# The sums of V are made chunk by chunk, between the score stages, instead of four in a row at the head of a super-chunk

## The chip, the cores and the metric

One Trainium2 chip, 8 of its cores, each with one of the eight sequences of the batch; nothing is exchanged between them. The metric is the time of one execution in device microseconds, that of the slowest core. Engines: PE (TensorE) multiplies matrices, ACT (ScalarE) evaluates functions, DVE (VectorE) reduces and copies, POOL (GpSimd) issues part of the DMAs here, and SP issues the others. The engines run beside each other, each through its own instructions in order, and wait for each other through semaphores.

## The reference, cut to what matters

```python
xn = _layernorm(x)                       # x: 8 x 8192 x 1024, one of the 8 per core
q, k, v = proj(xn)                       # 16 heads of 64, 64 chunks of 128 tokens
s_intra = q @ k.T * scale                # inside a chunk: 128 x 128 per head
intra   = softmax(s_intra) @ v
k_means = k.mean(over a chunk); v_means = v.mean(over a chunk)
s_inter = q @ k_means.T * scale          # against the means of chunks 0..c
inter   = softmax(s_inter, causal) @ v_means
attn    = (intra + inter) @ wo.T + bo
ffn     = gelu((xn @ U1) @ V1 + b1) @ U2 @ V2 + b2
out     = x + attn + ffn
```

## The kernel before, in words

A core goes through its 8192 tokens in 16 super-chunks (`sc`) of 512 tokens, that is four chunks of 128 (`cc` = 0 to 3, `c = 4 * sc + cc`). Every engine's instructions stand in the order in which the Python code emits them with `pm.do(engine, instruction, waits, incs)`; "t" is PE, "v" DVE, "s" ACT, "y" SP and "g" POOL. A wait stops the engine and all that is emitted behind it for that engine.

In each super-chunk: the normalized x is transposed (L399, L408), the projections of q and k (L424, copied by ACT at L433) and of v (L443 and L451, copied by DVE at L457 into `v_tm`) follow. DVE then sums the next super-chunk's x (`emit_ln_sums`, L337 and L340; not in the last super-chunk) and makes the chunk means of k with 32 pairs of small instructions, 8 pairs for each chunk (L473 and L478, into `km_fm`).

**The sums of v** (L483 to L514) stand next. For each chunk two matmuls with a column of ones (L489, L494) make one row of 1024 sums in PSUM banks 6 and 7; ACT copies the two halves (L500, L503) into a row buffer; POOL issues two DMAs (L508, L511) that carry the row to partition c and to partition 64 + c of `vm_cm`. There are two row buffers, and they are no memory of their own: `vrow_slots` is partition 0 of `A1T` and partition 0 of `A2T`, the tiles that later hold the exponentials. Chunk 2 takes the buffer of chunk 0 again, so its matmuls wait for the DMAs of chunk 0 (`vrow_guard`), and chunk 3 likewise for those of chunk 1.

**P1** (`emit_p1`, called P1(cc) below) makes six banks of scores for one chunk (L542 for the scores inside the chunk, L570 for those against `km_fm`); its first matmul waits for `km_done[cc]`. ACT exponentiates (L553, L589), DVE sums (L557, L594), ACT takes two logarithms (L609, L611), and DVE makes `neglse` (L615). **The bounce** (`emit_lse_bounce`) transposes `neglse` on PE (L623), DVE makes two copies (L628, L631), and POOL sends them to DRAM and back as flat rows (L638, L641, then four times L653). **P2** (`emit_p2_av`) makes the transposed scores with the flat rows added, part 0 and part 1 with three banks each (L680 and L690, or L698 and L711); L690 and L698 wait for the flat rows. ACT exponentiates each bank into `A1T` (L722) or `A2T` (L728). Part 2, **AV**, multiplies with v (L754) and with `vm_cm` (L778) into banks 6 and 7, which DVE copies out (L790).

The order of emission is P1(0), bounce(0), the first FFN matmul (L807), then for each cc: P1(cc + 1), P2(cc) part 0, bounce(cc + 1), P2(cc) part 1, AV(cc). With cc = 3 there is no P1 and no bounce. P1, P2 and the bounce take their PSUM banks in turn from banks 0 to 5 (`pool_next`), and each use of a bank waits until the bank's last content was read. One turn of the loop takes 6 + 3 + 1 + 3 = 13 banks, so the third bank of part 1 is the one that the first exponential of part 0 has to free.

The exponentials of P2 wait for `vm_ready`, because they overwrite the row buffers: the counts of the two DMA semaphores after all four chunks. AV waits for `vm_ready` since it reads `vm_cm`. After the fourth AV come the layer norm of the next super-chunk, the GELU part of the FFN (L846, L854, L870) and the output (L900 to L924).

Of the kernel before, what the change touches and what calls it, by code (L numbers as in the profile page):

```python
# [71 lines left out]
def build_nc(nsc=NSC_FULL, debug=False):  # L72
# [98 lines left out]
    c_t = Ctr(nc, "c_t")  # L171
# [8 lines left out]
    d_vm = [Ctr(nc, "d_vm0"), Ctr(nc, "d_vm1")]  # L180
# [14 lines left out]
    for (dst, src) in ((ident, ident_c), (ident_b, identb_c), (ones2, ones2_c),  # L195
# [8 lines left out]
          waits=[c_v], incs=[(d_ffw, 16)])  # L204
# [18 lines left out]
          waits=[d_ffw], incs=[(c_v, 1)])  # L223
# [12 lines left out]
    for wi, (wsrc, dstT, scale_col) in enumerate(wlist):  # L236
        for fc in range(8):
# [4 lines left out]
                  waits=w_st, incs=[(d_st[slot], 16)])  # L242
            wts = [(d_st[slot], d_st[slot].n), (d_cst, d_cst.n),
                   (c_v, ev_after.get(("e", slot), dbg_v0))]
            for half in range(2):
                bank = B[slot * 2 + half]
                for eci in range(4):
# [6 lines left out]
                          waits=(wts if (half == 0 and eci == 0) else ()),  # L254
# [21 lines left out]
    with nc.Block("setup") as blk1:  # L276
# [7 lines left out]
          waits=[(c_v, setup_v)], incs=[(c_t, 1)])  # L284
    t_bias0 = c_t.n
    pm.do("g", dma("g", bias_r[0:8, :], bk_h.rearrange("(a t) -> a t", t=128)),
          waits=[(c_t, t_bias0)], incs=[(d_ffw, 16)])
    pm.do("t", lambda e: e.transpose(B[0][0:128, 8:16], bias_r[0:8, :], ident[0:8, 0:8]),
          waits=[(d_ffw, d_ffw.n)], incs=[(c_t, 1)])
# [3 lines left out]
          waits=[(c_t, t_bias1)], incs=[(c_v, 1)])  # L293
# [3 lines left out]
          waits=[(c_v, v_bias1)], incs=[(d_ffw, 16)])  # L297
    pm.do("t", lambda e: e.transpose(B[0][0:128, 16:48], bias_r[:], ident[0:32, 0:32]),
          waits=[(d_ffw, d_ffw.n), (c_v, v_bias1)], incs=[(c_t, 1)])
    pm.do("v", lambda e: e.tensor_copy(b1_f[:], B[0][:, 16:48]),  # L300
          waits=[c_t], incs=[(c_v, 1)])
# [11 lines left out]
    vm_ready = [(d_vm[0], 0), (d_vm[1], 0)]  # L313
# [63 lines left out]
    for sc in range(nsc):  # L377
# [3 lines left out]
        if sc + 1 < nsc:  # L381
# [5 lines left out]
                  waits=[x_guard[npar]], incs=[(d_xp[npar], 16)])  # L387
# [3 lines left out]
        for st in range(4):  # L391
            bks = (4, 5) if st % 2 else (6, 7)
            for half in range(2):
                bk = bks[half]
                w = [(c_v, ln_done[st]), bank_free[bk]]
                for eci in range(4):
# [7 lines left out]
                          waits=(w if eci == 0 else ()),  # L404
# [9 lines left out]
                      waits=[(c_t, bank_gen[bk]), xnfm_guard], incs=[(c_v, 1)])  # L414
# [3 lines left out]
        for (wT, dst, brow) in ((wqT, q_fm, bq_eff), (wkT, k_fm, bk_f)):  # L418
            for fc in range(8):
                bk = fc % 4  # L420
                w = [(c_v, xn_ready), bank_free[bk], (c_s, setup_s)]
                for ec in range(8):
# [6 lines left out]
                          waits=(w if ec == 0 else ()),  # L429
# [5 lines left out]
                      waits=[(c_t, bank_gen[bk]), kq_guard], incs=[(c_s, 1)])  # L435
                bank_free[bk] = (c_s, c_s.n)
        for st in range(4):
            for half in range(2):
                bk = (st * 2 + half) % 4
                w = [(c_v, xn_ready), bank_free[bk]]  # L440
                for ec in range(8):
# [7 lines left out]
                          waits=(w if ec == 0 else ()))  # L449
# [10 lines left out]
                      waits=[(c_t, bank_gen[bk]), kq_guard], incs=[(c_v, 1)])  # L460
# [19 lines left out]
                      waits=[c_v], incs=[(c_v, 1)])  # L480
            km_done.append(c_v.n)

        for cc in range(4):  # L483
            c = 4 * sc + cc
            vr = vrow_slots[cc % 2]
            w = [(c_v, v_done), bank_free[6], bank_free[7], vrow_guard[cc % 2],
                 hflat_guard, a_guard]
            pm.do("t", (lambda cc=cc: lambda e:
                        e.matmul(B[6][0:1, :], ones_col[:],  # L489
                                 v_tm[:, cc * 1024:cc * 1024 + 512],  # L490
                                 start=True, stop=True))(),
                  waits=w, incs=[(c_t, 1)])
            pm.do("t", (lambda cc=cc: lambda e:
                        e.matmul(B[7][0:1, :], ones_col[:],  # L494
                                 v_tm[:, cc * 1024 + 512:cc * 1024 + 1024],
                                 start=True, stop=True))(),
                  incs=[(c_t, 1)])
            bank_gen[6] = bank_gen[7] = c_t.n
            pm.do("s", (lambda vr=vr: lambda e:
                        e.activation(vr[0:1, 0:512], B[6][0:1, :], AF.Copy))(),  # L500
                  waits=[(c_t, c_t.n)], incs=[(c_s, 1)])
            pm.do("s", (lambda vr=vr: lambda e:
                        e.activation(vr[0:1, 512:1024], B[7][0:1, :], AF.Copy))(),  # L503
                  incs=[(c_s, 1)])
            bank_free[6] = bank_free[7] = (c_s, c_s.n)
            sw = [c_s.snap()]
            pm.do("g", (lambda c=c, vr=vr: lambda e:
                        e.dma_start(out=vm_cm[c:c + 1, :], in_=vr))(),  # L508
                  waits=sw, incs=[(d_vm[cc % 2], 16)])
            pm.do("g", (lambda c=c, vr=vr: lambda e:  # L510
                        e.dma_start(out=vm_cm[64 + c:65 + c, :], in_=vr))(),  # L511
                  incs=[(d_vm[cc % 2], 16)])
            vrow_guard[cc % 2] = (d_vm[cc % 2], d_vm[cc % 2].n)
        vm_ready = [(d_vm[0], d_vm[0].n), (d_vm[1], d_vm[1].n)]  # L514

        cix = lambda h: (h % 2) * 8 + h // 2
        grp_heads = [[h for h in range(16) if cix(h) // 4 == g] for g in range(4)]
# [143 lines left out]
        def emit_p2_av(cc, flat_v, part):  # L661
# [11 lines left out]
            for kind, g in gens:  # L673
                bk = pool_next()
                if kind == "i":
                    for qi, h in enumerate(grp_heads[g]):
                        base = (h % 2) * 64
                        fc = h // 2
                        pm.do("t", (lambda bk=bk, qi=qi, base=base, fc=fc,
                                    cc=cc: lambda e: e.matmul(  # L680
                                        B[bk][:, qi * 128:(qi + 1) * 128],
                                        k_fm[base:base + 64, fc * 512 + cc * 128:
                                             fc * 512 + cc * 128 + 128],
                                        q_fm[base:base + 64, fc * 512 + cc * 128:
                                             fc * 512 + cc * 128 + 128],
                                        start=(qi == 0), stop=False,
                                        skip_group_check=True))(),
                              waits=([bank_free[bk]] if qi == 0 else ()))
                    pm.do("t", (lambda bk=bk, g=g, fi=fi, o2=o2: lambda e:
                                e.matmul(B[bk][:], o2,  # L690
                                         fi[:, g * 512:(g + 1) * 512],
                                         start=False, stop=True,
                                         skip_group_check=True))(),
                          waits=[(d_lsl, flat_v)], incs=[(c_t, 1)])
                else:
                    par8 = g
                    pm.do("t", (lambda bk=bk, g=g, fb=fb, s4=s4: lambda e:
                                e.matmul(B[bk][:], s4,  # L698
                                         fb[:, g * 512:(g + 1) * 512],
                                         start=True, stop=False,  # L700
                                         skip_group_check=True))(),
                          waits=[bank_free[bk], (d_lsl, flat_v)])
                    hs = [h for h in range(16) if h % 2 == par8]
                    for j, h in enumerate(hs):
                        base = (h % 2) * 64
                        fc = h // 2
                        q8 = cix(h) % 8
                        sl = (q8 % 4) * 128
                        pb = 64 * (q8 // 4)
                        pm.do("t", (lambda bk=bk, sl=sl, pb=pb, base=base,  # L710
                                    fc=fc, cc=cc, ncj=ncj, j=j: lambda e: e.matmul(  # L711
                                        B[bk][pb:pb + ncj, sl:sl + 128],
                                        km_fm[base:base + 64,
                                              fc * 64:fc * 64 + ncj],
                                        q_fm[base:base + 64, fc * 512 + cc * 128:
                                             fc * 512 + cc * 128 + 128],
                                        start=False, stop=(j == 7),
                                        skip_group_check=True))(),
                              incs=([(c_t, 1)] if j == 7 else ()))
                if kind == "i":  # L720
                    pm.do("s", (lambda bk=bk, g=g: lambda e:
                                e.activation(A1T[:, g * 512:(g + 1) * 512],  # L722
                                             B[bk][:], AF.Exp))(),
                          waits=[(c_t, c_t.n), avd] + vm_ready,
                          incs=[(c_s, 1)])
                else:
                    pm.do("s", (lambda bk=bk, g=g: lambda e:
                                e.activation(A2T[:, g * 512:(g + 1) * 512],  # L728
                                             B[bk][:], AF.Exp))(),
                          waits=[(c_t, c_t.n), avd] + vm_ready,  # L730
                          incs=[(c_s, 1)])
                exp_done[(kind, g)] = c_s.n
                bank_free[bk] = (c_s, c_s.n)
# [5 lines left out]
            for h in [hh for hh in range(16) if hh % 2 == 0] + \  # L739
# [10 lines left out]
                if ci % 4 == 0:  # L750
# [9 lines left out]
                      waits=w)  # L760
# [37 lines left out]
                bank_free[abk] = (c_v, c_v.n)  # L798

        nl0 = emit_p1(0)  # L800
        fl0 = emit_lse_bounce(0, nl0)
        flat_v = {0: fl0}
        for rc in range(2):
# [16 lines left out]
        for cc in range(4):  # L820
            if cc + 1 < 4:
                nl = emit_p1(cc + 1)
            exp_done_st[0] = {}
            emit_p2_av(cc, flat_v[cc], 0)
            if cc + 1 < 4:
                flat_v[cc + 1] = emit_lse_bounce(cc + 1, nl)
            emit_p2_av(cc, flat_v[cc], 1)
            emit_p2_av(cc, flat_v[cc], 2)
# [164 lines left out]
```

How the kernel before makes its waits and increments, by code:

```python
            def run(engine):  # L51
                done = {}
                for (ek, waits, fn, incs) in self.steps:
                    if ek != eng_key:
                        continue
                    for (c, val) in waits:
                        if val > 0 and done.get(id(c), -1) < val:
                            engine.wait_ge(c.h, val)
                            done[id(c)] = val
                    instr = fn(engine)
                    for (c, k) in incs:
                        instr.then_inc(c.h, k)
```

## Time and profile before

| what | value |
|---|---|
| median of 3 runs | 3536.42 us (3533.74 to 3555.97) |
| the profiled execution: its time | 3534.85 us |
| the profiled execution: span of its slowest core (5) | 3533.3 us |
| spans of the 8 cores | 3524.1 to 3533.3 us |
| granted TensorE clock of the 8 cores | 0.782 to 0.788 |
| busy: PE, ACT, DVE, POOL | 2437.2, 1208.0, 1056.0, 298.1 us |
| one super-chunk | about 207 to 215 us |

All times in rows are microseconds from the start of the span of core 5. The time of an execution is 1.55 us more than the span, which leaves out what lies before the first and after the last instruction.

### The profile page before, as it was taken

What the parts mean: (1) busy time and instruction counts of PE and PEld (TensorE: products, weight loads), DVE (VectorE), ACT (ScalarE), POOL (GpSimd) and SP (SyncE); (2) the same over time, 40 slices, a digit from 0 to 9 for tenths busy, and PEclk for the clock granted to TensorE, in tenths of its full rate; (3) what the DMA queues carried; (4) which work ended last, traced back from release to release, by engine and by line L of the source; (5) the groups of instructions that cost most, each with busy time, mean ns of one, the idle gap of its engine ahead of it and who ended that gap; (6) DMA issues with size and microseconds to landing.
All of it is one profiled execution on the core that took longest, in us unless ns stands there. A gap on an engine that the chain in (4) does not pass through costs nothing.

```text
span 3533.3 us, 41208 instructions; the slowest of 8 cores (3524.1 to 3533.3 us)
## 1 busy us (share of the span) xinstructions
PE 2437.2 (69%) x14403; PEld 1137.3 (32%) x14403; DVE 1056.0 (30%) x2444; ACT 1208.0 (34%) x2080; POOL 298.1 (8%) x558
## 2 busy tenths in 40 slices
PE   1267858676785767768576785867768576785867
PEld 0224333332333323333332333323333232333333
DVE  2432241413214141331513224141331513224141
ACT  0126143242513325252332614324252342614333
POOL 1101010100101010010100101010010100101010
PEclk9986959687695977859687695977859687695978
DMA  7400101000010100101010010100101010010000
GB/s 119 85 1 2 48 3 48 2 19 30 3 48 3 48 2 13 37 2 49 3 43 6 2 48 3 48 2 13 37 2 48 2 34 16 2 48 3 24 2 25
DMA packets 45429, 86.05 MB, mean 24 GB/s; under 512 B 17292, under 2 KB 24108, under 8 KB 44972
## 3 DMA queue, kind: packets, MB, share of 16 engines
q1 hardware_dynamic: 18348, 67.24, 5.4%
q0 software_dynamic: 26880, 16.18, 3.3%
q8 instruction: 120, 1.97, 0.2%
q14 instruction: 81, 0.66, 0.1%
HBM read 62.03 MB, written 34.60 MB: 27 GB/s over the span
## 4 chain that ended last, share of the span: by engine, by line
PE 56%; DVE 20%; issue 8%; ACT 7%; DMA 2%; POOL 1%; DVEq 1%; ACTq 0%; POOLq 0%
PE B L424 14%; PE B L870 7%; PE B L900 7%; PE B L443 7%; PE B L846 6%; DVE kcol L473 4%; DVE z L557 4%; PE B L807 3%; DVE km_fm L478 2%; PE B L690 2%; ACT v_tm L356 2%; DVE out_st L924 2%; DVE stats L337 2%; PE B L680 2%; PE B L754 2%
## 5 line engine op out<-in xcount | busy, mean ns | idle before, releaser
L870 PE MATMUL B<-H_rot,U 128*128 128x512 bf16 x1024 | 320.3, 399 | 134.9 <-ACT H_rot L854 133.8
L854 ACT ACTIVATE H_rot<-B,b_f 128x512 bf16<-128x512 f32 x512 | 349.2, 689 | 115.0 <-PE B L846 114.9
L433 ACT ACTIVATE q_fm<-B,bq_eff 128x512 bf16<-128x512 f32 x128 | 88.2, 689 | 730.6 <-PE B L424 730.6
L900 PE MATMUL B<-woT,attn_fm 128*128 128x512 bf16 x1024 | 242.6, 379 | 136.1 <-DVE out_st L924 111.2
L846 PE MATMUL B<-P_fm,V 128*128 128x512 bf16 x1024 | 332.3, 415 | 0.0
L623 PE MATMUL B<-identity,neglse 128*32 128x128 f32 x64 | 23.8, 371 | 401.3 <-DVE neglse L615 401.3
L457 DVE CAST v_tm<-B 128x512 bf16<-128x512 f32 x128 | 88.5, 691 | 678.6 <-PE B L451 678.6
L424 PE MATMUL B<-xn_fm,wqT 128*128 128x512 bf16 x1024 | 257.5, 418 | 31.9 <-DVE xn_fm L408 31.9
L443 PE MATMUL B<-wvT,xn_fm 128*128 128x512 bf16 x1024 | 243.0, 380 | 0.0
L424 PE MATMUL B<-xn_fm,wkT 128*128 128x512 bf16 x1024 | 223.6, 379 | 0.0
L553 ACT ACTIVATE B<-B,cvals 128x512 f32<-128x512 f32 x256 | 158.5, 659 | 182.1 <-PE B L542 181.9
L722 ACT ACTIVATE A1T<-B 128x512 bf16<-128x512 f32 x256 | 146.8, 592 | 161.4 <-PE B L690 161.4
L924 DVE TENSOR_TENSOR out_st<-B,x_buf 128x512 f32<-128x512 f32 x128 | 88.5, 692 | 376.7 <-PE B L917 376.7
L508 POOL DMA_DIRECT2D vm_cm<-A1T x32 | 16.0, 499 | 2122.1 <-ACT A1T L503 1986.7
L690 PE MATMUL B<-H_rot,ones 2*128 2x512 bf16 x256 | 147.3, 575 | 68.6 <-DMA Q_fm<-lse_scr 57.8
L870 PEld LDWEIGHTS B<-H_rot,U 128*128 128x128 bf16 x1024 | 101.4, 101 | 278.2 <-issue 173.2
L790 DVE CAST attn_fm<-B 128x512 bf16<-128x512 f32 x128 | 82.4, 686 | 341.1 <-PE B L778 341.1
L900 PEld LDWEIGHTS B<-woT,attn_fm 128*128 128x128 bf16 x1024 | 91.1, 97 | 265.2 <-issue 174.5
L557 DVE TENSOR_REDUCE z<-B 128x4 f32<-128x512 f32 x256 | 164.9, 685 | 16.8 <-ACT B L553 14.9
L589 ACT ACTIVATE B<-B,cvals 128x8 f32<-128x8 f32 (+42 forms) x128 | 58.1, 454 | 322.1 <-DVE z L557 322.1
L886 DVE CAST Q_fm<-B 128x512 bf16<-128x512 f32 x32 | 20.6, 685 | 483.6 <-PE B L870 483.6
L424 PEld LDWEIGHTS B<-xn_fm,wqT 128*128 128x128 bf16 x1024 | 107.1, 106 | 177.2 <-issue 79.8
(104 smaller groups left out, 3241.9 us busy)
## 6 DMA issues: line engine op xcount, KB each, us to landing
x_buf<-L_attn_hidden_states SPq DMA_DIRECT2D x16, 2048.0 KB, 10.2
out<-out_st SPq DMA_DIRECT2D x64, 512.0 KB, 2.7
V<-L_ffn_V POOLq DMA_DIRECT2D x1, 2048.0 KB, 23.9
U<-L_ffn_U POOLq DMA_DIRECT2D x1, 2048.0 KB, 40.3
H_rot<-L_attn_wq POOLq DMA_DIRECT2D x8, 256.0 KB, 4.0
H_rot<-L_attn_wk POOLq DMA_DIRECT2D x8, 256.0 KB, 3.8
H_rot<-L_attn_wv POOLq DMA_DIRECT2D x8, 256.0 KB, 3.8
H_rot<-L_attn_wo POOLq DMA_DIRECT2D x8, 256.0 KB, 3.8
```

What stands on the lines that cost most here:

```text
L424: e.matmul(B[bk][:], wT[:, ec * 1024 + fc * 128: ec * 1024 + fc * 128 + 128], xn_fm[:, ec * 512:(ec + 1) * 512], start=(ec == 0), stop=(ec ...
L443: e.matmul(B[bk][:], xn_fm[:, ec * 512 + st * 128: ec * 512 + st * 128 + 128], wvT[:, ec * 1024 + half * 512: ec * 1024 + half * 512 + 512 ...
L473: e.reduce_sum(kcol[:], k_fm[:, fc * 512 + cc * 128: fc * 512 + cc * 128 + 128], axis=AX.X))(),
L553: e.activation(B[bk][:], B[bk][:], AF.Exp, bias=cvals[:, 5:6]))(),
L557: e.reduce_sum(z1[:, 4 * g:4 * g + 4], B[bk][:].rearrange("p (a b) -> p a b", a=4), axis=AX.X))(),
L690: e.matmul(B[bk][:], o2, fi[:, g * 512:(g + 1) * 512], start=False, stop=True, skip_group_check=True))(),
L722: e.activation(A1T[:, g * 512:(g + 1) * 512], B[bk][:], AF.Exp))(),
L846: pm.do("t", (lambda bk=bk, g=g, rc=rc: lambda e: e.matmul(B[bk][:], V1[:, rc * 4096 + g * 128:rc * 4096 + g * 128 + 128], P_fm[:, rc * 51 ...
L854: pm.do("s", (lambda bk=bk, g=g: lambda e: e.activation(H_rot[:, (g % 4) * 512:(g % 4) * 512 + 512], B[bk][:], AF.Gelu_apprx_tanh, bias=b1 ...
L870: pm.do("t", (lambda gq=gq, rc=rc: lambda e: e.matmul(B[6 + rc][:], U2[:, gq * 256 + rc * 128:gq * 256 + rc * 128 + 128], H_rot[:, (gq % 4 ...
L900: e.matmul(B[bk][:], attn_fm[:, ec * 512 + st * 128: ec * 512 + st * 128 + 128], woT[:, ec * 1024 + half * 512: ec * 1024 + half * 512 + 512],
L924: lambda e: e.tensor_tensor(out_st[:, slot * 1024 + half * 512: slot * 1024 + half * 512 + 512], B[bk][:], xb[:, st * 1024 + half * 512: s ...
```

## The change

The loop over the four sums of v becomes a function `emit_vsum(cc)`. It is called for chunk 0 right after P1(0), and for chunk cc + 1 right after P1(cc + 1), ahead of P2(cc) part 0. `vm_latest[0]` holds the counts of the DMA semaphores after the newest call, and the exponentials of P2 wait for these. `vm_ready`, for which AV waits, is now that of its own chunk. Nothing is computed otherwise, and the number of instructions of each kind stays.

```diff
-        for cc in range(4):
+        vm_latest = [[(d_vm[0], 0), (d_vm[1], 0)]]
+
+        def emit_vsum(cc):
             c = 4 * sc + cc
             vr = vrow_slots[cc % 2]
             w = [(c_v, v_done), bank_free[6], bank_free[7], vrow_guard[cc % 2],
...
             vrow_guard[cc % 2] = (d_vm[cc % 2], d_vm[cc % 2].n)
-        vm_ready = [(d_vm[0], d_vm[0].n), (d_vm[1], d_vm[1].n)]
+            vm_latest[0] = [(d_vm[0], d_vm[0].n), (d_vm[1], d_vm[1].n)]
+            return vm_latest[0]
...
                     pm.do("s", (lambda bk=bk, g=g: lambda e:
                                 e.activation(A1T[:, g * 512:(g + 1) * 512],
                                              B[bk][:], AF.Exp))(),
-                          waits=[(c_t, c_t.n), avd] + vm_ready,
+                          waits=[(c_t, c_t.n), avd] + vm_latest[0],
                           incs=[(c_s, 1)])
                 else:
                     pm.do("s", (lambda bk=bk, g=g: lambda e:
                                 e.activation(A2T[:, g * 512:(g + 1) * 512],
                                              B[bk][:], AF.Exp))(),
-                          waits=[(c_t, c_t.n), avd] + vm_ready,
+                          waits=[(c_t, c_t.n), avd] + vm_latest[0],
                           incs=[(c_s, 1)])
...
         nl0 = emit_p1(0)
+        vm_ready_cc = {0: emit_vsum(0)}
         fl0 = emit_lse_bounce(0, nl0)
...
         for cc in range(4):
             if cc + 1 < 4:
                 nl = emit_p1(cc + 1)
+                vm_ready_cc[cc + 1] = emit_vsum(cc + 1)
+            vm_ready = vm_ready_cc[cc]
             exp_done_st[0] = {}
             emit_p2_av(cc, flat_v[cc], 0)
```

## Rows read from the trace of the kernel before

**Rows 1.** The page: busy time, and the chain that ended last by engine.
```profile
PE 2437.2 (69%) x14403; PEld 1137.3 (32%) x14403; DVE 1056.0 (30%) x2444; ACT 1208.0 (34%) x2080; POOL 298.1 (8%) x558
PE 56%; DVE 20%; issue 8%; ACT 7%; DMA 2%; POOL 1%; DVEq 1%; ACTq 0%; POOLq 0%
```
**Rows 2.** Timeline of PE, head of the fifth super-chunk: start, length, instruction, [idle before].
```profile
1061.10 0.38 PE L489 MATMUL B<-v_tm,ones_col 128*1 128x512 bf16 x1 [1.05 <-DVE v_tm L457]
1068.13 0.58 PE L489 MATMUL B<-v_tm,ones_col 128*1 128x512 bf16 x1 [4.12 <-DMA vm_cm<-A1T]
...
1072.81 1.01 PE L542 MATMUL B<-k_fm,q_fm 64*128 64x128 bf16 x8 [1.25 <-DVE km_fm L478]
...
1094.16 0.37 PE L623 MATMUL B<-identity,neglse 128*32 128x128 f32 x1 [19.16 <-DVE neglse L615]
```
**Rows 3.** Timeline of DVE, the same stretch.
```profile
1067.55 0.29 DVE L473 TENSOR_REDUCE kcol<-k_fm 128x1 f32<-128x128 bf16 x1 [0.37 <-DVE stats L340]
...
1088.61 1.29 DVE L557 TENSOR_REDUCE z<-B 128x4 f32<-128x512 f32 x2
```
**Rows 4.** Timeline of PE, turn cc = 1 of this super-chunk, and L690 of cc = 3.
```profile
1112.48 1.03 PE L542 MATMUL B<-k_fm,q_fm 64*128 64x128 bf16 x8
...
1119.54 0.37 PE L623 MATMUL B<-identity,neglse 128*32 128x128 f32 x1 [1.58 <-DVE neglse L615]
...
1121.45 0.60 PE L698 MATMUL B<-Q_fm,sel 4*128 4x512 bf16 x1
1121.99 0.60 PE L711 MATMUL B<-q_fm,km_fm 64*18 64x128 bf16 x8
1122.52 1.49 PE L754 MATMUL B<-A1T,v_tm 128*64 128x128 bf16 x16
1123.94 0.67 PE L778 MATMUL B<-A2T,vm_cm 18*64 18x128 bf16 x16
1124.55 1.03 PE L542 MATMUL B<-k_fm,q_fm 64*128 64x128 bf16 x8
...
1140.16 0.58 PE L690 MATMUL B<-H_rot,ones 2*128 2x512 bf16 x1 [2.90 <-DMA Q_fm<-lse_scr]
```
**Rows 5.** Timeline of ACT: copies of v sums, then the turn of rows 4.
```profile
1062.29 0.57 ACT L503 ACTIVATE A1T<-B 1x512 bf16<-1x512 f32 x1
...
1069.23 0.59 ACT L500 ACTIVATE A1T<-B 1x512 bf16<-1x512 f32 x1 [4.06 <-PE B L494]
1069.73 0.57 ACT L503 ACTIVATE A1T<-B 1x512 bf16<-1x512 f32 x1
...
1118.74 0.29 ACT L611 ACTIVATE lnz<-z,cvals 128x16 f32<-128x16 f32 x1
1118.94 1.06 ACT L722 ACTIVATE A1T<-B 128x512 bf16<-128x512 f32 x2
1119.90 0.60 ACT L728 ACTIVATE A2T<-B 128x512 bf16<-128x512 f32 x1
```
**Rows 6.** Timeline of POOL: its DMA issues (start, length) in the same super-chunk.
```profile
1065.91 0.52 POOL L508 DMA_DIRECT2D vm_cm<-A1T  x1 [135.46 <-ACT A2T L503]
1066.42 0.53 POOL L511 DMA_DIRECT2D vm_cm<-A1T  x1
...
1070.83 0.49 POOL L508 DMA_DIRECT2D vm_cm<-A1T  x1 [2.94 <-ACT A1T L503]
1071.31 0.48 POOL L511 DMA_DIRECT2D vm_cm<-A1T  x1
...
1133.45 0.51 POOL L638 DMA_DIRECT2D lse_scr<-rows_cd  x1 [6.84 <-PE B L690]
```
**Rows 7.** The tile vm_cm: from issue to landing of its 128 DMAs.
```profile
DMA to landing us min/median/max: 1.5/1.6/2.8
```
**Rows 8.** Line L553, its table loads: ns, first and last start.
```profile
L553 ACT ACT_TABLE_LOAD  x15: 1283/1283/1283, 449.8 to 3394.5; - x15
```
**Rows 9.** Timeline of ACT: last of P1(0), first of P1(1).
```profile
1093.37 0.29 ACT L611 ACTIVATE lnz<-z,cvals 128x16 f32<-128x16 f32 x1
1101.12 1.24 ACT L553 ACTIVATE B<-B,cvals 128x512 f32<-128x512 f32 x2 [7.46 <-PE B L542]
```

## Prediction, made before the changed kernel was run

> **What bounds the kernel now.** I read the page first. PE is busy for 69% of the span, but the chain that ended last gives it only 56%, with 20% to DVE and 8% to issue [rows 1]. So there are stages in which PE waits, and the change lies in two of them: the head of a super-chunk and the loop over the chunks. I then read the timelines of PE, DVE, ACT and POOL through one super-chunk, the fifth; I write S for the start of a P1 on PE.
>
> *The head.* The four sums of v start on PE at 1061.10, the third is held up by 4.12 us for the DMA of the first, and P1(0) starts at 1072.81. That looks like 11.7 us of work ahead of P1(0). But the row of P1(0) names DVE's `km_fm` as what ended its wait, and PE had been idle for 1.25 us by then [rows 2]. And P1(0) isn't what is late: its first bank's sum (L557) starts on DVE at 1088.61, after 32 pairs for the means of k that run without a gap since 1067.55, and PE's transpose comes at 1094.16 after 19.16 us of idleness [rows 2, 3]. DVE sets the end of this stage.
>
> *The loop.* A turn is a closed chain. P1(2) starts at 1112.48 and P1(3) at 1124.55, 12.07 us later [rows 4]. Inside it: scores, exponentials, sums, logarithms (L611 at 1118.74), `neglse`, the transpose L623 at 1119.54 for which PE has waited 1.58 us, then part 1 of P2, AV from 1122.52, and the next P1. What ACT does right after L611, the exponentials of part 0 from 1118.94 on [rows 5], is needed only when PE gets to the third bank of part 1 at 1121.45 [rows 4], since that bank is the one which the first exponential frees. In turn cc = 3 there is no P1; there PE waits 2.90 us for flat rows from DRAM [rows 4].
>
> **The change, part by part.**
>
> *Removed from the head:* 8 matmuls, 8 copies and 8 DMA issues. Worth nothing: DVE's run of 1067.55 to 1088.61 does not depend on them, and L557 can't start sooner [rows 3]. P1(0) itself keeps its start, as it waits for `km_fm` [rows 2]. If that cover were gone, up to the 11.7 us of the head would be won (first rival).
>
> *Chunk 0's sum behind P1(0):* its matmuls fall into PE's 19.16 us of idleness [rows 2]. Its copies stand behind L611 (1093.37), where ACT has 7.46 us to spare [rows 9]. Its two issues take about 1 us of POOL ahead of bounce(0)'s L638, which may come some 0.2 us late. Nothing waits for that: in turn 0 PE has slack before its transpose as in turn 1. I take 0.
>
> *Chunks 1 to 3 behind P1(1) to P1(3), on PE:* two matmuls of 0.4 to 0.6 us [rows 2] in a turn in which PE afterwards waits 1.58 us for L623 [rows 4]. 0. Banks 6 and 7 are free for them once DVE has copied the last AV, during P1.
>
> *The same on ACT, POOL and the queue: a new wait.* In order on ACT stand now L611, L500, L503, and then the first exponential of part 0, which waits for `vm_latest`: for the DMAs of the row that ACT has only just written. Step by step from S:
> - L611 is followed by the next instruction at 1118.94, that is S + 6.46 [rows 5].
> - Two copies: from 1069.23 to 1069.73 + 0.57 = 1070.30, that is 1.07. S + 7.53 [rows 5].
> - POOL starts L508 at 1070.83, 0.53 after that; L511 follows 0.48 later [rows 6]. S + 8.54.
> - From the start of L511 (1066.42) to the PE instruction that waited for it (1068.13) it is 1.71 us [rows 2, 6], in line with 1.5 to 2.8 us, median 1.6, for all of these DMAs [rows 7]. S + 10.25.
>
> So the first exponential starts at S + 10.25 instead of S + 6.46: 3.79 us late. Queued behind it on ACT are the other five of the chunk and then those of the next P1; PE waits for them. Of these 3.79 us a part is slack. The first exponential lasts about 0.6 us, to S + 10.85. With 0.1 us to PE, L698 starts at S + 10.95 instead of 1121.45, which is S + 8.97. It and L711 take 1.07 us (1121.45 to 1122.52), so AV starts at S + 12.02 instead of S + 10.04: **2.0 us late**. The rest of ACT's row keeps up: exponentials follow every 0.48 us (three from 1118.94 to 1119.90, rows 5), so that AV's third group of heads, at S + 12.73, finds its exponential ended at about S + 12.3, and the last bank's is ended at about S + 13.3, ahead of L778's second half at S + 13.8. The next P1 follows AV at once, so the turn is longer by 2.0 us.
>
> What the three turns with a new wait cost:
> - cc = 0 and cc = 1: 2.0 us each. In turn 0 the same steps hold.
> - cc = 2: AV ends 2.0 us late too, but what comes next on the path is L690 of cc = 3, for which PE waits 2.90 us for flat rows [rows 4]. Those depend on P1(3) and the bounce, not on AV. So the 2.0 us fall into this gap, with 0.9 us to spare. If that cover were gone, they would cost 2.0.
> - cc = 3: no new sum. But the flat rows come from L638, which now stands behind L508 and L511 of chunk 3 on POOL. By the steps above (P1(3) at 1124.55) these end at 1124.55 + 8.54 + 0.48 = 1133.57, and L638 started at 1133.45 [rows 6]. 0.1 to 0.2 us late, on the path: 0.15.
>
> **The sum**: 2.0 + 2.0 + 0.15 = 4.15 us for each super-chunk, x 16 = 66 us. On the profiled execution's 3534.85 us that is 3601; it lies 1.6 us below the median of the runs, so I forecast **3602 us**, 1.9% slower.
>
> The landing is the least sure of the terms. The Trainium skill, "DMA: Bandwidth & Descriptors", section "Anatomy of one DMA — SWDGE (gpsimd) path", puts a DMA issued by POOL at about 2.0 us plus its bytes over 436 GB/s, 2.0 us for such a row. By it each of the 32 waits that count would be 0.3 us longer and the time some 9 us more; the trace's 1.71 us has been used.
>
> **The bounds of the unknown terms.** The landing is 1.5 to 2.8 us [rows 7], against 1.71 used: -7 to +35 us over 32 waits. POOL's start after the copy: 0.53 us is what most of these issues show; the first in this super-chunk took 3.05 us (copy ended at 1062.29 + 0.57 = 1062.86, L508 at 1065.91), but after 135 us of idleness [rows 5, 6], which the moved ones of chunks 1 to 3 don't have. If the slack of cc = 2 were used up by something else: +32. If one of the two paying turns found a cover that I don't see: -33.
>
> **Rivals.**
>
> *Faster: the chain of v sums was what held up the head.* If the sums' 11.7 us stood on the path, 16 x 11.7 = 187 us would be won and 66 lost: 3415 us. It decides from the point where `km_fm` and L557 don't wait for DVE. Against it: the PE row names DVE, and DVE runs without a gap for 21 us after [rows 2, 3]. 0.03.
>
> *Same: the new wait is covered.* If the first exponential of part 0 had 3.8 us of slack or more, instead of the 1.8 that I find, all would lie beside the chain: 3536 to 3540 us. For it speaks that ACT is busy only 34% of the time [rows 1]. Against it, the bank that has to come free and AV right behind. 0.08.
>
> *Slower still: ACT changes its function tables.* L500 and L503 are copies that now stand between logarithm and exponential. If each pair needed a table of its own, three turns would have two loads of 1.283 us [rows 8] each; the second lies beside the DMA, the first delays the copies: 32 x 1.28 = 41 us, 3643 us, and more if cc = 2's cover gives way. Against it: only 15 loads at L553 for 16 super-chunks, the first at 449.8 [rows 8]; in the first super-chunk the copies ran ahead of L553 with the table of the layer norm's logarithm and exponential, and L553 needed no load. 0.04.
>
> *Slower still: the 2.0 us of cc = 2 come through.* 66 + 32 = 98 us: 3634 us. Against it the 2.90 us. 0.08.
>
> **How the numbers follow.** My forecast has the rest, 0.77. Its own range, from the bounds of the landing and half a turn's cover, is 3580 to 3632 us, and the other cases lie outside or at its edge; the range is 3580 to 3632. About 1% is what a measurement of this kernel can tell from no change. Faster by over 1% is the first rival, 0.03; within 1% (3501 to 3572) the second, with a little for a forecast that comes out at less than half: 0.09; slower 0.88.
>
> **What would show it.** Right: in the changed profile ACT's L722 waits for a DMA of `vm_cm` three times in each super-chunk, for about 2.7 us each; L698 of part 1 waits on ACT; a turn cc = 1 takes 14.0 instead of 12.07 us; the wait of L690 in cc = 3 for flat rows shrinks from 2.9 to about 1 us; POOL's waits for the copies stay. The stretch from the last v copy to L557 stays as it is, and P1(0) still waits for `km_fm`. Wrong: P1(0)'s first L557 comes sooner, ACT shows more than 32 table loads, or PE's L698 doesn't wait. The step most open is how much of the 3.79 us is slack.

## The result, and the profile after

The changed kernel is slower: 1.0209 times the kernel before, 95% interval 1.0181 to 1.0237. Some executions of every kernel here ran with a lower granted clock on one die; they are left out of all ratios and of the times given for each kernel. The kernel before lies at 3534 to 3556 us and the changed one, all but one execution of 3629, at 3607 to 3612 us. The profiled execution took 3609.12 us where the one before took 3534.85: 74.3 us more, where the forecast was 66. The new line numbers are those of before plus 2 or 3 in P1, P2 and the bounce (L690 is L693, L698 is L701, L722 is L725, L638 is L641), and plus 4 to 6 behind.

First the page: busy times and the chain, as in [rows 1].

```profile
PE 2463.4 (68%) x14403; PEld 1138.9 (32%) x14403; DVE 1057.0 (29%) x2444; ACT 1189.6 (33%) x2080; POOL 301.5 (8%) x558
PE 55%; DVE 19%; issue 8%; ACT 8%; DMA 3%; POOL 2%; DVEq 1%; ACTq 0%; POOLq 0%
```

The same instructions in the same number; no engine has gained work that comes near to 74 us. (PE's busy time is up by 26 us; `own_rows2` below, with its matmuls in the same places and without the wait, has 2433.1.) What grew in the chain is ACT, DMA and POOL, by 1% each. That is waiting, and the list of waits names it (who waited for whom: us in total, times, longest):

```profile
ACT A1T L725 <- DMA vm_cm<-A2T: 89.1, 32, 3.5
PE B L701 <- ACT A1T L725: 70.4, 48, 2.2
ACT A1T L725 <- DMA vm_cm<-A1T: 44.8, 16, 3.5
```

Neither ACT nor L698 had such a wait before. There are 48 of each, three in each super-chunk: ACT's are 2.8 us long on the mean (133.9 / 48), and half of that, 1.47 us (70.4 / 48), is handed on to PE. Now one turn, cc = 1 of the fifth super-chunk, on PE (timeline; compare [rows 4]):

```profile
1138.40 1.03 PE L545 MATMUL B<-k_fm,q_fm 64*128 64x128 bf16 x8
...
1145.46 0.37 PE L626 MATMUL B<-identity,neglse 128*32 128x128 f32 x1 [1.21 <-DVE neglse L618]
...
1149.36 0.58 PE L701 MATMUL B<-Q_fm,sel 4*128 4x512 bf16 x1 [1.39 <-ACT A1T L725]
1149.87 0.61 PE L714 MATMUL B<-q_fm,km_fm 64*18 64x128 bf16 x8
1150.41 1.51 PE L757 MATMUL B<-A1T,v_tm 128*64 128x128 bf16 x16
1151.85 0.67 PE L781 MATMUL B<-A2T,vm_cm 18*64 18x128 bf16 x16
1152.46 1.03 PE L545 MATMUL B<-k_fm,q_fm 64*128 64x128 bf16 x8
...
1168.18 0.58 PE L693 MATMUL B<-H_rot,ones 2*128 2x512 bf16 x1 [0.96 <-DMA Q_fm<-lse_scr]
```

and the same turn on ACT (compare [rows 5]) and on POOL (compare [rows 6]):

```profile
1144.86 0.57 ACT L502 ACTIVATE A1T<-B 1x512 bf16<-1x512 f32 x1
1145.34 0.57 ACT L505 ACTIVATE A1T<-B 1x512 bf16<-1x512 f32 x1
1148.62 1.08 ACT L725 ACTIVATE A1T<-B 128x512 bf16<-128x512 f32 x2 [2.71 <-DMA vm_cm<-A1T]
```
```profile
1146.46 0.51 POOL L510 DMA_DIRECT2D vm_cm<-A1T  x1 [8.34 <-ACT A1T L505]
1146.96 0.52 POOL L513 DMA_DIRECT2D vm_cm<-A1T  x1
1147.46 0.52 POOL L641 DMA_DIRECT2D lse_scr<-rows_cd  x1
...
1160.63 0.51 POOL L510 DMA_DIRECT2D vm_cm<-A2T  x1 [8.01 <-ACT A2T L505]
1161.13 0.52 POOL L513 DMA_DIRECT2D vm_cm<-A2T  x1
1161.63 0.52 POOL L641 DMA_DIRECT2D lse_scr<-rows_cd  x1
```

With S = 1138.40 the reader can lay the forecast's steps beside the rows:

| step | forecast, from S | measured |
|---|---|---|
| copies begin behind the logarithm | 6.46 | 1144.86: 6.46 |
| copies end | 7.53 | 1145.91: 7.51 |
| second issue begins | 8.54 | 1146.96: 8.56 |
| first exponential | 10.25 | 1148.62: 10.22 |
| third bank of part 1 on PE | 10.95 | 1149.36: 10.96 |
| AV | 12.02 | 1150.41: 12.01 |
| next P1 | 14.0 | 1152.46: 14.06 |

The head (timelines of PE, then DVE, fifth super-chunk; compare [rows 2, 3]):

```profile
1096.37 1.01 PE L545 MATMUL B<-k_fm,q_fm 64*128 64x128 bf16 x8 [12.87 <-DVE km_fm L478]
1098.49 0.59 PE L491 MATMUL B<-v_tm,ones_col 128*1 128x512 bf16 x1
...
1117.62 0.37 PE L626 MATMUL B<-identity,neglse 128*32 128x128 f32 x1 [18.12 <-DVE neglse L618]
```
```profile
1083.60 0.69 DVE L457 CAST v_tm<-B 128x512 bf16<-128x512 f32 x1 [1.46 <-PE B L451]
...
1112.07 1.29 DVE L560 TENSOR_REDUCE z<-B 128x4 f32<-128x512 f32 x2
```

Before, P1(0) began 11.7 us behind the first sum of v, with 1.25 us of waiting for `km_fm`. With the sums gone it waits 12.87 us for the same `km_fm`. From the end of the last copy of v (1084.29) to L560 it is 27.8 us; before it was 1060.84 to 1088.61, also 27.8. What was taken out of the head has turned into idleness of PE.

To see a whole kernel at a time, I read the starts of P1, the transpose and AV on PE in all 16 super-chunks from the timeline of the slowest core, and took sums over the 16 (us):

| kernel | P1(0) to its transpose | turn cc = 0 | turn cc = 1 | P1(3) to AV(3) |
|---|---|---|---|---|
| before | 342.2 | 194.6 | 198.7 | 335.0 |
| after | 343.5 | 228.0 | 231.8 | 335.5 |
| difference | 1.3 | 33.4 | 33.1 | 0.5 |

A turn is from one P1 to the next. The two turns carry 66.5 of the 74.3 us. In the first column the last super-chunk has 2.7 us more and the fifteen others 0.1 us less each: in the last, DVE has no sums of x to make and the sums of v had held P1(0) back, so it now begins sooner, and its transpose is as late as before. In the rest, the first P1 of the execution comes at 244.0 instead of 240.9 us, and the parts between AV(3) and the next P1(0) are 3.0 us longer over the 16.

Most of these last 6 us are not the change's. The table compares core 5 before with core 3 after, and both figures differ that much among the cores of one execution. The mean over all eight cores is 3528.7 us before and 3599.5 after, that is 70.8 us more. Of these the two turns have 32.5 and 33.1, P1(3) to AV(3) 2.3 (333.7 and 336.0), the first P1 0.9 (243.1 and 244.0), and the part behind AV(3) together with P1(0) to P1(1) 2.1 (2558.8 and 2560.9).

### The profile page after: what moved, and what is told of

It is laid out like the page before. It is cut to its first block, busy times and chain, and to the rows that moved or that the text cites. A ratio compares the mean times of both kernels' runs of the same rounds, so it can differ in the third digit from the quotient of the medians.

```text
span 3607.6 us, 41287 instructions; the slowest of 8 cores (3591.3 to 3607.6 us)
## 1 busy us (share of the span) xinstructions
PE 2463.4 (68%) x14403; PEld 1138.9 (32%) x14403; DVE 1057.0 (29%) x2444; ACT 1189.6 (33%) x2080; POOL 301.5 (8%) x558
## 4 chain that ended last, share of the span: by engine, by line
PE 55%; DVE 19%; issue 8%; ACT 8%; DMA 3%; POOL 2%; DVEq 1%; ACTq 0%; POOLq 0%
PE B L424 13%; PE B L876 7%; PE B L906 7%; PE B L443 6%; PE B L852 6%; DVE kcol L473 4%; DVE z L560 4%; PE B L811 3%; DVE km_fm L478 2%; ACT v_tm L356 2%; DVE out_st L930 2%; DVE stats L337 2%; PE B L757 2%; PE B L916 2%; PE B L693 2%
## 5 line engine op out<-in xcount | busy, mean ns | idle before, releaser
L545 PE MATMUL B<-k_fm,q_fm 64*128 64x128 bf16 x1024 | 116.3, 283 | 197.8 <-DVE km_fm L478 197.8
L725 ACT ACTIVATE A1T<-B 128x512 bf16<-128x512 f32 x256 | 143.4, 605 | 206.2 <-DMA vm_cm<-A2T 89.1
L560 DVE TENSOR_REDUCE z<-B 128x4 f32<-128x512 f32 x256 | 165.1, 686 | 16.7 <-ACT B L556 14.9
L693 PE MATMUL B<-H_rot,ones 2*128 2x512 bf16 x256 | 147.5, 576 | 27.1 <-DMA Q_fm<-lse_scr 17.0
```

What stands on the lines that cost most here:

```text
L560: e.reduce_sum(z1[:, 4 * g:4 * g + 4], B[bk][:].rearrange("p (a b) -> p a b", a=4), axis=AX.X))(),
L693: e.matmul(B[bk][:], o2, fi[:, g * 512:(g + 1) * 512], start=False, stop=True, skip_group_check=True))(),
L725: e.activation(A1T[:, g * 512:(g + 1) * 512], B[bk][:], AF.Exp))(),
```

## The experiments

Four questions: is it ACT's wait, or the work put into the turns; does each wait cost alike; was the head worth anything; and what would make it so. The kernel before ran beside each, mostly at 3531 to 3547 us. On the chip of `own_rows2`, `kl_after` and `kl_head_own4` it varied more, from 3534 to 3586.

**The rows get a buffer of their own** (`own_rows`, and once more as `own_rows2`). Nothing of the change is moved back; only the reason for the exponentials to wait is taken away.

```diff
-    bv_row = sb("bv_row", [1, 1024], BF16)
+    bv_row = sb("bv_row", [128, 1024], BF16)
...
-    vrow_slots = {0: A1T[0:1, 0:1024], 1: A2T[0:1, 0:1024]}
+    vrow_slots = {0: bv_row[32:33, :], 1: bv_row[64:65, :]}
...
-                          waits=[(c_t, c_t.n), avd] + vm_latest[0],
+                          waits=[(c_t, c_t.n), avd],
...
-                          waits=[(c_t, c_t.n), avd] + vm_latest[0],
+                          waits=[(c_t, c_t.n), avd],
```

> The changed kernel, but the rows of v sums have a buffer of their own (partitions 32 and 64 of the tile that holds the v bias), so the exponentials of P2 need not wait for any DMA of the sums. Same matmuls, copies and DMA issues, in the same places. My theory (the new wait of ACT is the whole cost): the turns cc = 0 and 1 are back to 11.5 to 13.1 us and the time is that of the kernel before, 3536 to 3545 us. Rival (the work put into the turns costs, not the wait: matmuls on PE, copies on ACT, issues on POOL): it stays at 3595 to 3610 us. Rival (the head was worth something and the wait hid it): clearly under 3536.

3541 to 3547 us, one at 3578; 1.0045 times the kernel before (1.0018 to 1.0072). So about 64 of the 74 us hang on the wait (58 by the two ratios). The matmuls, copies and issues stand in the turns as in the changed kernel, so the first rival falls. The second falls too: nothing is faster than before. A remainder of 6 to 10 us stays between the usual executions (6 to 25 by the interval of the ratio), and the second run was made to look for it.

> own_rows once more, for a profile that can be read beside that of the kernel before: own_rows came out at 1.0045 of it, some 8 us above what it should be if the wait were the whole cost. My theory: L638 behind the sum's issues on POOL costs 0.15 to 0.2 us in turn cc = 3 of each super-chunk (about 3 us), the rest stands in no turn; the turns cc = 0 and 1 are those of the kernel before within 0.05 us. Rival (the matmuls or copies cost in the turns): 0.1 us or more in each of 32 turns.

Again 3541 to 3549 us, one at 3585; the ratio is 0.9992, but from 0.9921 to 1.0064 and beside a kernel before that varied from 3534 to 3586 us itself, so the first run's ratio is the better one. Its profile: the turns add up to 194.8 and 200.1 us, against 194.6 and 198.7 before. Typical turns are the same within 0.02 us (12.07 in the fifth super-chunk in both); the 1.4 us of difference in turn cc = 1 is one turn, that of the twelfth super-chunk, of 14.27 us in place of 12.71. So the rival (0.1 us or more in each turn) is out. P1(3) to AV(3) takes 338.7 against 335.0 us. On the mean of the eight cores the remainder is 8.1 us (3536.8 and 3528.7), with 4.2 of them in P1(3) to AV(3) and 1.5 in turn cc = 1. The typical super-chunk has 0.35 us more from P1(3) to AV(3), in the direction that L638 behind the two issues would give. The profile has one thing more (waits of POOL: us in total, times, longest):

```profile
POOL lse_scr L641 <- issue: 9.1, 5, 2.9
```

Five times POOL starts late for no reason that the profile shows. The kernel before has such starts too, three of them (its waits of POOL):

```profile
POOL vm_cm L508 <- issue: 8.6, 2, 4.3
POOL H_rot L641 <- issue: 4.4, 1, 4.4
```

There two fell on the sums of v at the head, where nobody waited. The third fell on bounce(3) of the eleventh super-chunk, where P1(3) to AV(3) takes 23.4 us and its neighbours take 20.8 and 21.2. In `own_rows2` they fall on other bounces. One start, 2.83 us late, is followed by the flat rows for the one long turn (timelines of POOL and PE):

```profile
2592.78 0.51 POOL L641 DMA_DIRECT2D lse_scr<-rows_cd  x1 [2.83 <-issue]
2592.84 1.03 PE L545 MATMUL B<-k_fm,q_fm 64*128 64x128 bf16 x8
...
2599.90 0.58 PE L693 MATMUL B<-H_rot,ones 2*128 2x512 bf16 x1 [3.21 <-DMA Q_fm<-lse_scr]
```

Another, 2.91 us late, precedes the flat rows of cc = 2 in the eighth super-chunk, whose stretch from P1(3) to AV(3) is 1.5 us longer than before. Both are there on all eight cores. So these two starts make up about 3 of the 8 us; the rest is the 0.35 us above, less what the kernel before lost in its eleventh super-chunk, and small differences outside the turns.

**Only chunk 3's sum is moved** (`move3`; 0 to 2 at the head):

```diff
-        nl0 = emit_p1(0)
-        vm_ready_cc = {0: emit_vsum(0)}
+        vm_ready_cc = {}
+        for hc in range(3):
+            vm_ready_cc[hc] = emit_vsum(hc)
+        nl0 = emit_p1(0)
...
-                vm_ready_cc[cc + 1] = emit_vsum(cc + 1)
+                if cc + 1 >= 3:
+                    vm_ready_cc[cc + 1] = emit_vsum(cc + 1)
```

> The changed kernel, but the sums of chunks 0, 1 and 2 stand at the head as before; only chunk 3's is made in the loop, behind P1(3). Shared row buffers, so ACT waits for the DMA of this row in turn cc = 2 alone. My theory: AV(2) is 2 us late, but falls into PE's wait of 2.9 us for the flat rows of cc = 3: 3536 to 3545 us. Rival (each such wait costs its 2 us): 3536 + 33 = 3569 us. Rival (bounce(3) late by more than 0.2 us behind the sum's two issues on POOL): 3550 or more.

3544 to 3545 us in five of seven, 1.0043 (1.0021 to 1.0064). The wait is there, 16 times (list of waits, from an execution of 3668 us; only the count and the length of the waits are read from it):

```profile
ACT A1T L725 <- DMA vm_cm<-A2T: 44.3, 16, 3.2
```

2.8 us each, 44.3 in all, and hardly 9 of them reach the end: the slack of cc = 3 covers the rest. The rival's 3569 is out. That of 3550 or more is not out by the ratio alone (3543 to 3559 us), though five of the seven lie under it.

**The sums of chunks 2 and 3 are moved** (`move23`, the same with 2 for 3):

> As before, but the sums of chunks 2 and 3 are both in the loop, 0 and 1 at the head. ACT waits in turns cc = 1 and cc = 2. My theory: only cc = 1 pays, 2.07 us x 16: 3536 + 33 + 2 = 3571 us. Rival (each sum in the loop costs the same third of the whole): 3536 + 49 = 3585 us. Rival (the cost comes in turn cc = 0, where the FFN matmul stands): 3540.

3573 to 3576 us in three of four, 1.0127 (1.0089 to 1.0165). Turn cc = 0 adds up to 194.4 us, as before; turn cc = 1 to 231.4, that is 32.7 more or 2.05 each. The rivals expected 3585 and 3540. The 37 to 40 us are the one turn that pays, plus the remainder that all these kernels have.

**Exact waits** (`precise`): each exponential waits only for the row in its own tile.

```diff
-                          waits=[(c_t, c_t.n), avd] + vm_latest[0],
+                          waits=[(c_t, c_t.n), avd] + vm_latest[0][0:1],
...
-                          waits=[(c_t, c_t.n), avd] + vm_latest[0],
+                          waits=[(c_t, c_t.n), avd] + vm_latest[0][1:2],
```

> The changed kernel with exact waits: the exponentials into A1T wait only for the DMAs of the row in A1T, those into A2T only for those of the row in A2T. In turn cc = 0 the newest row is in A2T, so only the third and later exponentials of the chunk are late; in turn cc = 1 it is in A1T, as late as before. My theory (a wait costs what comes after the slack of its own exponential): turn 0 costs about 1.0 us instead of 2.07, turn 1 2.07: 3609 - 17 = 3592 us. Rival (it is the lateness of the DMA that counts, whoever waits for it): 3609 us. Rival (turn 0 pays nothing): 3576 us.

3591 us in the profiled execution; the only other one that counts took 3618, so the ratio is wide, 1.0193 (1.0144 to 1.0242), and the verdict rests on the turns. Timeline of ACT in turn cc = 0 of the fifth super-chunk:

```profile
1124.46 0.57 ACT L505 ACTIVATE A2T<-B 1x512 bf16<-1x512 f32 x1
1124.94 1.05 ACT L725 ACTIVATE A1T<-B 128x512 bf16<-128x512 f32 x2
1127.87 0.60 ACT L731 ACTIVATE A2T<-B 128x512 bf16<-128x512 f32 x1 [1.89 <-DMA vm_cm<-A2T]
```

The two exponentials into A1T run at once, the one into A2T waits, and with it those behind. Turn 0 takes 1.0 us more than before in 12 of the 16 super-chunks (12.49 in place of 11.49 in the first) and about 2 in the other four, together 21.0 us more in place of the 33.4 of the changed kernel; turn 1 stays at 231.6. It is 12 us less than the changed kernel's turns, where I expected 17; the mean of the eight cores gives 13 (213.7 and 227.0). The same DMA, as late as before, costs half when what it blocks has more slack. The long turns I can't explain: those of the eighth and tenth super-chunk are long on all eight cores, the others on some.

**The head alone** (`head_own4`): the kernel before, with the four sums at the head and a row buffer for each, so that the third does not wait for a DMA. The exponentials lose their wait for `vm_ready` too.

```diff
-    vrow_slots = {0: A1T[0:1, 0:1024], 1: A2T[0:1, 0:1024]}
+    vrow_slots = {0: bv_row[32:33, :], 1: bv_row[64:65, :], 2: bv_row[96:97, :],
+                  3: bob2_row[32:33, :]}
...
-            vr = vrow_slots[cc % 2]
+            vr = vrow_slots[cc]
```

> The kernel before with the four sums at the head, but each with a row buffer of its own (no wait of chunk 2 for the DMA of chunk 0, and none of the exponentials for the DMAs). My theory (the head ends when DVE has made the means of k, so the sums of v are worth nothing there): 3536 us, within 5. Rival (the sums hold the head up): about 2 to 4 us less in each super-chunk, 3470 to 3505 us.

3534 to 3540 us in five of eight, three at 3551 to 3586, 1.0024 (0.9986 to 1.0062). PE's wait for the DMA at the head is gone and nothing is won.

**DVE's work at the head is cut** (`km_before`): the kernel before with one reduction and one scaling for each chunk's means of k.

```diff
-            for fc in range(8):
-                pm.do("v", (lambda fc=fc, cc=cc: lambda e:
-                            e.reduce_sum(kcol[:], k_fm[:, fc * 512 + cc * 128:
-                                                       fc * 512 + cc * 128 + 128],
-                                         axis=AX.X))(),
...
+            pm.do("v", (lambda cc=cc: lambda e:
+                        e.reduce_sum(kcol[:], k_fm[:, 0:4096].rearrange(
+                            "p (fc t) -> p fc t", fc=8)[
+                                :, :, cc * 128:cc * 128 + 128],
+                                     axis=AX.X))(),
```

> The kernel before with one thing changed on DVE: the means of k are made with one reduction of 128 x 8 x 128 and one scaling for each chunk, instead of 8 pairs. 4 pairs at about 1.6 us instead of 32 at 0.65 us: 14.5 us less on DVE at the head. My theory (DVE alone sets the end of the head, up to the point where something else ends last): 3536 - 16 x 14.5 = 3304 us. Rival (the sums of v hold the head up nearly as long): 3350 us or more.

3312 to 3322 us, 0.9369 (0.9329 to 0.9410). A pair now looks like this (timeline of DVE, a later super-chunk):

```profile
1219.36 1.22 DVE L472 TENSOR_REDUCE kcol<-k_fm 128x8 f32<-128x1024 bf16 x1
1220.68 0.19 DVE L478 TENSOR_SCALAR km_fm<-kcol 128x8 bf16<-128x8 f32 x1
1220.98 1.22 DVE L472 TENSOR_REDUCE kcol<-k_fm 128x8 f32<-128x1024 bf16 x1
```

1.62 us in place of 8 times 0.65, and the time follows by 214 to 224 us, 13.4 to 14.0 in each super-chunk where I expected 14.5. DVE was what bound the head.

**And the sums for the layer norm are spread** (`kl_before`): as `km_before`, and each of the four reductions of the next x (L337) stands behind one of the four bounces.

```diff
-        if sc + 1 < nsc:
-            ln_sums_next = emit_ln_sums(sc + 1)
...
         fl0 = emit_lse_bounce(0, nl0)
+        if sc + 1 < nsc:
+            ln_sums_next = emit_ln_sums(sc + 1, [0])
...
                 flat_v[cc + 1] = emit_lse_bounce(cc + 1, nl)
+                if sc + 1 < nsc:
+                    ln_sums_next = emit_ln_sums(sc + 1, [cc + 1])
```

> As km_before, and the four sums of the next super-chunk's x are taken out of the head and put on DVE behind the four bounces, one each, where DVE is idle. Now DVE's work at the head is 6.4 us and the four sums of v, 8 us and more up to P1(0), end last. My theory: the first sum of scores comes about 10.6 us after the last copy of v instead of 27.8 us: 3536 - 15 x 17.2 - 10.8 = 3267 us. Rival (the moved sums cost their 1.6 us in each turn): 3267 + 16 x 4 = 3330 us or more.

3285 to 3294 us and one at 3314, 0.9306 (0.9252 to 0.9361): some 20 us above my sum, and below the rival's. From the last copy of v to the first sum of scores it is 11.5 us on the mean of the heads, not 10.6, which is some 14 of the 20. The turns are not longer (195.0 and 198.9 us), so the reductions do fit in. Now the sums of v are the last thing ahead of P1(0) (timeline of PE: L492 is the second matmul of a sum, L540 the first of P1(0), with no wait before it):

```profile
1195.62 0.63 PE L492 MATMUL B<-v_tm,ones_col 128*1 128x512 bf16 x1
1196.18 1.03 PE L540 MATMUL B<-k_fm,q_fm 64*128 64x128 bf16 x8
```

**The change on this footing, with its own buffers** (`kl_own`) **and with the shared ones** (`kl_after`):

> The changed kernel with row buffers of its own (as own_rows), and DVE's work as in kl_before. My theory: with DVE no longer last, the place of the sums of v counts. P1(0) starts about 2 us after the last copy of v, DVE's means end at 6.5 us, and the first sum of scores follows them instead of coming at 10.6: 4.1 us less than kl_before in each super-chunk, about 3200 us. Rival (the head stays bound by something else): the same as kl_before.

> The changed kernel with its shared row buffers, and DVE's work as in kl_before and kl_own. My theory: the move wins at the head what kl_own won, and loses 2.05 us in each of 32 turns: kl_own's 3206 to 3216 + 66 = about 3275 us, hardly less than kl_before (3285). Rival (with another head the wait finds cover): near kl_own.

`kl_own`: 3206 to 3220 us, 0.9074 (0.9030 to 0.9118), the fastest of all: 79 us less than `kl_before` between the lowest of each, both on one chip, where I expected 66. P1(0) waits for `km_fm` alone again, 42.6 us over 16 heads:

```profile
PE B L543 <- DVE km_fm L475: 42.6, 16, 2.7
```

`kl_after`: 3265 us twice and once 3302, 0.9249 (0.9142 to 0.9356). Its turns add up to 226.4 and 231.3 us, 61 more than those of `kl_own` (196.6 and 199.8), and its lowest time, on another chip, is 59 us above: the wait costs here nearly what it costs in the change. The move with its own buffers wins 79, and the wait takes 59 of it back.

**The own buffers without the move** (`kl_head_own4`):

> kl_before with the sums of v at the head and a row buffer of its own for each of the four, so the third no longer waits for a DMA. It parts what kl_own won into the move and the buffer. My theory (the move did most of it): about 1.5 to 2 us less at the head of each super-chunk than kl_before, 3255 to 3262 us. Rival (the own buffers did it, the place is of no matter): about 3210 us.

Only two executions count, 3306 and 3319 us: 0.9348 (0.9272 to 0.9424), not below `kl_before` and above my 3255 to 3262. Whole times can't part the 79 us, so I read the profiles. Cores 0 to 3 of this kernel have spans of 3254.5 to 3262.8 us, cores 4 to 7 of `kl_before` 3278.2 to 3280.0, all at granted clocks of 0.806 to 0.809: about 19 us less. The cores of `kl_own` have 3192 to 3204. The head itself, from the end of the last copy of v to the transpose of P1(0) on PE, adds up over the 16 super-chunks to (one core each):

| kernel | core | head, us |
|---|---|---|
| before | 5 | 528.4 |
| after | 3 | 528.6 |
| `head_own4` | 3 | 528.7 |
| `km_before` | 0 | 298.9 |
| `kl_before` | 4 | 279.0 |
| `kl_head_own4` | 0 | 264.3 |
| `kl_own` | 1 | 197.6 |
| `kl_after` | 4 | 197.5 |

With DVE as it was, neither the move nor the buffers change the head. With DVE's work cut, the buffers alone win 14.7 us of it, 0.9 in each super-chunk where I expected 1.5 to 2, and the move with them 81.4. So the larger part of the 79 us is the move's.

## Why the prediction was right, point by point

The changed kernel came out at 1.0209; 3602 us is 1.0185 of the median before, and the sum was 66 where the profiled executions differ by 74.3 us and the mean spans of their eight cores by 70.8.

- *The head is worth nothing.* Right: 27.8 us from the last copy of v to L557 in both; `head_own4` wins nothing; `km_before` shows who was the bound.
- *The new wait, step by step to S + 10.25.* Right within 0.03 us at each step. The landing, the least sure term, was 1.66 us from the second issue (1146.96) to ACT (1148.62), where 1.71 had been used. The Trainium skill's 2.0 us for such a DMA ("DMA: Bandwidth & Descriptors", section "Anatomy of one DMA — SWDGE (gpsimd) path") is not what this trace shows: by an estimate from its figure the exponential would have come 0.3 us later than it did.
- *How much of it is slack.* The step that I called most open. Right: AV at S + 12.01 for 12.02. `precise` shows from the other side that it is the slack behind the wait that sets the price.
- *Two turns pay, the third is covered.* Right: 33.4 and 33.1 us in turns 0 and 1 for 32 each, in cc = 3 the wait of L690 fell from 2.90 to 0.96 us, and `move3` and `move23` show each half alone.
- *L638 late by 0.15 us in cc = 3.* Right on the whole. In the fifth super-chunk L641 of bounce(3) starts at 1161.63, S + 9.17 for P1(3) at 1152.46, where it was S + 8.90 [rows 4, 6], which is 0.27 us late. Over the 16 super-chunks the issue comes 2.9 us later after its P1(3) in total, 0.18 on the mean, where the sum had 2.4. P1(3) to AV(3) is 2.3 us longer on the mean of the eight cores. The table's 0.5 for the slowest core hides a typical 0.28 us in each super-chunk, because the kernel before lost about 2.3 us to the late start of POOL in its eleventh.
- *What the sum lacked.* The turns' excess over 64, 2.5 us, comes from single long turns. In the turn of 15.54 us (the thirteenth super-chunk) ACT waited 3.48 us, since the DMA landed 2.43 us after its issue (2868.58 to 2871.01); on all eight cores that turn takes 15.3 to 15.6 us. Outside the two turns and P1(3) to AV(3) the slowest cores differ by 7.3 us and the mean of the eight cores by 3.0; the other 4 come from comparing two different cores. Why that DMA lands late, and what the 3.0 us are, I leave open.
- *The rivals.* ACT loads 32 tables after as before (16 at L854, 15 at L553, one at L356), so copies between logarithm and exponential need none. The other three are answered above.

## What to carry to other kernels

Before moving work off a stage, ask which engine ends that stage: here PE had 1.25 us of idleness left behind the sums of v, and DVE was busy for another 16 us, so the place freed was worth nothing. It was worth something only when DVE's 32 pairs were cut to 4 and its sums of x were moved away; the move was not tried with the first of these cuts alone. When a small buffer is borrowed from a tile that is written next, the distance between filling it, draining it by DMA, and overwriting the tile is part of its price; brought close together they cost copies, issues and landing, here 3.8 us, less the slack behind. And price such a wait through the engine that consumes the blocked result: the same wait cost 2.05, about 1.0 or, in cc = 2, at most 0.3 us, by what stood behind it.

## What the runs showed of the hardware that I had not expected

- One reduction over 128 x 8 x 128 takes 1.22 us where eight over 128 x 128 take 8 x 0.29, and with their scalings (8 x 0.16) and the gaps of about 0.1 us between instructions that wait for each other 5.2 us in all. The same sums cost 3.6 us less by being made with 2 instructions instead of 16.
- POOL starts a few DMA issues in an execution 0.2 to 4.7 us late with no reason in the profile. Starts that are over 2 us late: 3 in the kernel before (4.3, 4.4 and 4.3 us), 3 in the changed one (3.0, 2.8 and 2.9). They go with the place in POOL's stream of instructions, not with the time. In the kernel before all three are there on all eight cores. In `after`, `precise`, `own_rows2` and `kl_own`, where POOL's instructions stand in the same order, it is the same three issues of the copy to `lse_scr` (L641, in `kl_own` L639), in the eighth, twelfth and sixteenth super-chunk, although the first of them comes at 1797, 1783, 1758 and 1591 us. Why is not shown. What such a start costs depends on the issue that it hits: nothing at the sums of v, about 2.3 us at a bounce(3), about 1.5 at the two of `own_rows2`.
